# Running column sums and maxima of a graph network: ScalarE copies landed columns into PSUM, VectorE combines one column at a time

## What is computed

```python
h = jnp.maximum(_layernorm(x), 0.0)
x = x + _L0(h)      # segment_sum(H[src] * norm, dst), relu
x = x + _L1(h, ...) # segment_sum(h[src] * Wij(edge_attr) * edge_weight, dst)
for l in range(4):  # _L2: theta/phi projections, then
    agg = jax.ops.segment_max(msg, dst, num_segments=n)
for k in range(2):  # _L3: GCN convolutions
    out = jax.ops.segment_sum(h[src] * norm[:, None], dst, num_segments=n) + b
```

## Time and profile before

| | us |
|---|---|
| median of 3 runs | 10545.39 (10544.9 to 10546.17) |
| span of the profiled execution | 10630.0 |
| the seven passes, each | 1145 to 1148 |
| the stage between passes 1 and 2 (update and layer 1) | 1871 |
| from one later pass to the next | 91 to 99 |

### The profile page before, as it was taken

How to read it: one execution, slowest core, us unless ns; L and a number is a source line. 1 busy time by engine, 2 the same in 40 slices (tenths; PEclk the granted TensorE clock), 3 DMA queues, 4 the chain that set the end, 5 groups by cost and what they waited for, 6 DMA issues and landing times. The chain is left out here.

```text
span 10630.0 us, 49732 instructions
## 1 busy us (share of the span) xinstructions
PE 1639.5 (15%) x9025; PEld 1437.8 (14%) x9025; DVE 4419.4 (42%) x9272; ACT 543.8 (5%) x1417; POOL 8032.4 (76%) x7137
## 2 busy tenths in 40 slices
PE   2000048888860000100001000100001000010000
PEld 1000047777750000100001000100001000010000
DVE  4444434444443444344443444334444444444444
ACT  2000021111130000000000000000001000000000
POOL 4777768888847777677776777777777777777777
PEclk7555567777775555555555555555555555555555
DMA  5444435555532333333333333323333333333333
GB/s 190 142 142 142 145 88 77 77 74 76 77 86 91 95 95 95 99 95 95 95 97 97 95 95 95 101 93 95 95 95 98 96 95 95 95 100 95 95 95 104
DMA packets 467313, 1064.01 MB, mean 100 GB/s; under 512 B 156534, under 2 KB 276192, under 8 KB 412586
## 3 DMA queue, kind: packets, MB, share of 16 engines
q0 software_dynamic: 320736, 464.07, 19.8%
q1 hardware_dynamic: 143480, 597.45, 15.5%
q10 hardware_dynamic: 2940, 1.00, 0.0%
HBM read 517.80 MB, written 552.72 MB: 101 GB/s over the span
## 5 line engine op out<-in xcount | busy, mean ns | idle before, releaser
L991 POOL DMA_INDIRECT WORK<-table,S x5824 | 6249.0, 1073 | 2037.5 <-issue 1772.7
L1045 DVE TENSOR_TENSOR Z<-WORK,RESET 128x512 f32<-128x512 f32 x612 | 423.5, 692 | 2615.7 <-DMA WORK<-table,S 2601.8
L1210 POOL DMA_INDIRECT acc<-TOT,stage x832 | 1300.8, 1564 | 276.0 <-issue 207.6
L1090 PE MATMUL bank<-ident,WORK 128*128 128x128 f32 x7 | 3.3, 474 | 8069.6 <-DVE WORK L1074 8069.6
L1045 DVE TENSOR_TENSOR Z<-WORK,KEEP 128x512 f32<-128x512 f32 x459 | 317.6, 692 | 1958.9 <-DMA WORK<-table,S 1948.5
L1090 PEld LDWEIGHTS bank<-ident,WORK 128*128 128x128 f32 x7 | 1.3, 183 | 8071.1 <-DVE WORK L1074 8071.1
L1048 DVE TENSOR_TENSOR WORK<-WORK,Z 128x512 f32<-128x512 f32 x1071 | 741.0, 692 | 36.5
L1064 DVE TENSOR_TENSOR WORK<-WORK,Z 128x1536 f32<-128x1536 f32 (+2 forms) x448 | 633.8, 1431 | 12.4
L1059 DVE TENSOR_TENSOR Z<-WORK,S 128x1536 f32<-128x1536 f32 (+2 forms) x448 | 633.6, 1431 | 12.3
L1415 DVE SCALAR_TENSOR_TENSOR BASE<-bank,WEIGHT,BASE 128x128 f32<-128x128 f32 x832 | 234.2, 344 | 839.8 <-PE bank L1285 772.3
L1053 DVE SCALAR_TENSOR_TENSOR WORK<-WORK,S 128x128 f32<-128x128 f32 x1428 | 502.5, 352 | 50.9
(11 more groups left out here) (247 smaller groups left out, 2663.4 us busy)
## 6 DMA issues: line engine op xcount, KB each, us to landing
run_rows<-WORK SPq DMA_DIRECT2D x357, 1024.0 KB, 4.1
WORK<-table,S POOLq DMA_INDIRECT x5824
fill_rows<-BASE SPq DMA_DIRECT2D x52, 1024.0 KB, 6.8
WORK<-fill_rows SPq DMA_DIRECT2D x104, 512.0 KB
table<-TF SPq DMA_DIRECT2D x56, 384.0 KB
WORK<-carry_rows SPq DMA_DIRECT2D x49, 384.0 KB
acc<-TOT,stage POOLq DMA_INDIRECT x832
acc<-Z SPq DMA_DIRECT2D x12, 1024.0 KB
```

Of the source, the lines that this page charges most:

```text
L991: pool.indirect_dma_start(RING_T[:, b * WIDE + k, :], None, table, table_row(table, INDEX[:, t:t + 1]))\
L1045: step(dve.tensor_tensor(TMP[:, 0:groups, 0, :], rows[:, :, j - 1, :], mask(keep[:, :, j], groups, 0), op0))
L1210: pool.indirect_dma_start(acc_dram[a], bass.IndirectOffsetOnAxis(stage[:, h, j % HALF:j % HALF + 1].bitcast(u32), 0), TOT[:, j // QUAD % 2 ...
```

## The change

ScalarE, after each four columns (a `QUAD`) have landed, copies them (128 x 512) from the ring to one of the eight PSUM banks, in turn. VectorE then does one SCALAR_TENSOR_TENSOR for each column: its first input is the column before in the ring (SBUF), its second the landed column in PSUM, its scalar one number per partition from `KEEP` or `RESET` (SBUF), its output the column's place in the ring. The chunks' TENSOR_TENSORs, the scratch and the masks fall away. `reduced` counts columns. A bank is copied into again when VectorE has done the last column that it held.

```diff
-        def prefix_masks(dve, st, maximum):
...
+            def act_part(act):
+
+                for q in range(T // QUAD):
+                    act.wait_ge(landed[q % len(landed)], base + 16 * QUAD * (q * QUAD // SPAN + 1))
+                    wait(act, reduced, (q - BANKS + 1) * QUAD)
+                    first = q * QUAD % SPAN
+                    act.copy(bank(q % BANKS), RING_T[:, first:first + QUAD, :].rearrange("p t f -> p (t f)"))\
+                        .then_inc(copied, 1)
...
-                    for j in range(1, FOUR):
-                        wait(dve, reduced, n)
-                        step(dve.tensor_tensor(TMP[:, 0:groups, 0, :], rows[:, :, j - 1, :],
-                                               mask(keep[:, :, j], groups, 0), op0))
-                        wait(dve, reduced, n)
-                        step(dve.tensor_tensor(rows[:, :, j, :], rows[:, :, j, :], TMP[:, 0:groups, 0, :], op1))
...
-                for c in range(LAST):
-                    combine(c * WIDE, GROUPS)
-                    assert n == done(c)
...
+                for t in range(T):
+                    q = t // QUAD
+                    if t % QUAD == 0:
+                        dve.wait_ge(copied, q + 1)
+                    wait(dve, reduced, t)
+                    dve.scalar_tensor_tensor(RING_T[:, t % SPAN, :], RING_T[:, (t - 1) % SPAN, :], scale[:, t:t + 1],
+                                             bank(q % BANKS)[:, t % QUAD * F:(t % QUAD + 1) * F], op0, op1)\
+                        .then_inc(reduced, 1)
...
-                        if k == WIDE - 1 and c >= RING - 1:
-                            wait(pool, reduced, done(c - RING + 1))
+                            wait(pool, reduced, t - SPAN + 2)
```

More of the change, by code:

```diff
@@ L44 @@
 RING = 64 // WIDE
-FOUR = 4
-GROUPS = WIDE // FOUR
+BANKS = 8
 COUNT = T // WIDE
@@ L224, in gnn_kernel @@
         INDEX = S[:, 0:T].bitcast(i32)
-        PREFIX = S[:, T:2 * T]
-        TMP = Z[:, 0:3 * GROUPS * F].rearrange("p (g j f) -> p g j f", g=GROUPS, j=3)
         RING_T = WORK[:, :].rearrange("p (t f) -> p t f", f=F)
@@ L250, in gnn_kernel @@
         src_turned, src_sb = sem("src_turned"), sem("src_sb")
-        staged, reduced = sem("staged"), sem("reduced")
+        staged, reduced, copied = sem("staged"), sem("reduced"), sem("copied")
         stored = [sem(f"stored{i}") for i in range(BUFS)]
@@ L822, in gnn_kernel @@
         clear()
-        def prefix_masks(dve, st, maximum):
-            st.then(dve.tensor_copy(PREFIX[:, 0:T:FOUR], KEEP[:, 0:T:FOUR]))
-            for j in range(1, FOUR):
-                st.then(dve.tensor_tensor(PREFIX[:, j:T:FOUR], PREFIX[:, j - 1:T:FOUR], KEEP[:, j:T:FOUR], ALU.mult))
-            if maximum:
-                st.then(dve.tensor_scalar(PREFIX, PREFIX, -1.0, BIG, ALU.add, ALU.mult))
         def run_ends(pool, index, g):
@@ L917, in rows @@
                         on_a(act, g)
+                before["act"](act)
                 if norm_x:
@@ L956, in _, with passing @@
                 sp.wait_ge(table_out, 16 * NG)
-        def passing(maximum, pbase, fill=False, masks=None):
+        def passing(maximum, pbase, fill=False):
             base = total.gathers
@@ L967, in passing @@
             carry_dram = carry_rows[1 if maximum else 0]
-            tail = ((WIDE - HALF, 8), (WIDE - HALF + 8, 6), (WIDE - 2, 2))
-            parts = (((0, WIDE - HALF),) if WIDE > HALF else ()) + tail
+            parts = ((0, 8), (8, 6), (14, 2))
             stored_all = [16 * len(range(b, LAST, RING)) + (16 * len(parts) if LAST % RING == b else 0)
                           for b in range(RING)]
[L972 to L981, removed]
             def pool_part(pool):
@@ L995, in pool_part @@
                     pool.wait_ge(stored[b], stored_all[b])
-            total_steps = done(LAST)
+            def act_part(act):
[5 more added lines that the diff above has]
+                        .then_inc(copied, 1)
             def carry_out(pool):
@@ L1076, in dve_part @@
-                assert n == done(LAST) == total_steps
+                for t in range(T):
[6 more added lines that the diff above has]
+                        .then_inc(reduced, 1)
@@ L1088, in pe_part @@
             def pe_part(pe):
-                pe.wait_ge(reduced, total_steps)
+                pe.wait_ge(reduced, T)
                 nc.tensor.transpose(bank(0)[:, 0:P], RING_T[:, (T - 1) % SPAN, :], ident[:]).then_inc(pe_done, 1)
@@ L1106, in sp_part @@
                     if fill:
-                        wait(sp, reduced, done(c - 1) if c else 0)
+                        wait(sp, reduced, c * WIDE)
                         for h in range(WIDE // HALF):
@@ L1111, in sp_part @@
                     for first, n in parts if c == LAST else [(0, WIDE)]:
-                        sp.wait_ge(reduced, done(c, first + n) if c == LAST else done(c))
+                        sp.wait_ge(reduced, c * WIDE + first + n)
                         store(c, first, n)
@@ L1121, in sp_part, with layer @@
                         sp.wait_ge(zeroed[h], 16 * ITERS)
-            return {"pool": pool_part, "dve": dve_part, "pe": pe_part, "sp": sp_part,
+            return {"pool": pool_part, "dve": dve_part, "pe": pe_part, "act": act_part, "sp": sp_part,
                     "carry_out": carry_out, "carry_clear": carry_clear}
-        def layer(maximum, index, post, norm_x, weights, finish, scatter=False, masks=None):
-            before = passing(maximum, total.patches, scatter, masks)
+        def layer(maximum, index, post, norm_x, weights, finish, scatter=False):
+            before = passing(maximum, total.patches, scatter)
             base = list(total.rows)
@@ L1185, in edgeconv_rows @@
             return on_v, on_a
-        layer(False, idx_sum, post_gcn(None), True, [WT[:, 1, :]], (None, plain_rows), scatter=True, masks=False)
+        layer(False, idx_sum, post_gcn(None), True, [WT[:, 1, :]], (None, plain_rows), scatter=True)
         QI = UNROLL // QUAD
@@ L1572, in gnn_kernel @@
             layer(True, idx_max, post_edgeconv(False), False, [WE[:, l, k * F:(k + 1) * F] for k in range(2)],
-                  edgeconv_rows(bias_e[:, l, :]), masks=True if l == 1 else None)
+                  edgeconv_rows(bias_e[:, l, :]))
         layer(True, idx_max, post_edgeconv(True), True, [W12[:, 0, :]], (gcn_rows, None))
-        layer(False, idx_sum, post_gcn(0), False, [W12[:, 1, :]], (gcn_rows, None), masks=False)
+        layer(False, idx_sum, post_gcn(0), False, [W12[:, 1, :]], (gcn_rows, None))
         last = passing(False, total.patches)
@@ L1603, in _ @@
                     dve.tensor_tensor(X[:, gsl(g), :], X[:, gsl(g), :], rows, ALU.add).then_inc(rows_used, 1)
+            @block.scalar
+            def _(act):
+                last["act"](act)
             @block.tensor
```

## The result

| | median us | runs | ratio to before, 95% interval |
|---|---|---|---|
| before | 10545.78 | 10544.9 to 10547.65 | |
| after | 9790.7 | 9790.5 to 9794.59 | 0.9284 [0.9271, 0.9297] |

A forecast was written before the change was run, and what follows sets the result against it. The prediction took GpSimd's gathers, plus what VectorE makes them wait, as the bound. From 10545.4 us it took 751 of waiting and added 6 for copies at pass ends: 9800, range 9780 to 9890.

The forecast's parts named there:

- The bound and the 751 us: Seven passes: GpSimd's gathers set the pace; their waits for VectorE, 5824 x (1073 - 944) ns, give 751 us to remove.
- `prefix_masks`, put at 0: Mask work at the start of three passes beside gathers, VectorE otherwise idle; removing it was to gain 0.
- The mechanism: A gather that begins while a VectorE instruction with two SBUF inputs runs stands still until that instruction ends.
- second rival: Gathers wait because VectorE is busy, whatever it reads: 461 us remain, 290 gained, about 10260; chance 0.03.
- third: Rival: DMA engines set the pace once gathers come without a break; no change but 6 us, 10551; chance 0.02.
- The column instruction: 832 new VectorE instructions per pass, about 344 to 352 ns each, hold up no gather: price nothing.
- first rival: Column instructions hold gathers in part: 175 us, so 9975; at worst 512 us, so 10312; chance 0.06.
- ScalarE's copy: Copy to PSUM taken as 0.80 us, exposed only at pass ends: about 0.85 with hand-over, 6 us over seven passes.
- From span to runs: The runs' median lies 84.6 us below the profiled span 10630.0; the same difference was taken off the result.
- last rival: ScalarE's copies hold gathers: 1456 x 0.80 = 1165 us replace the 751, so 10965, slower; chance 0.02.

The follow-up runs named there:

- e1: The kernel before the change, unedited, profiled once more: 10545.45 us.
- e9: Changed kernel plus one unneeded VectorE add per four columns, both inputs in SBUF, placed between first and second column: 10058.1 us, ratio 0.9525.
- e10: Changed kernel plus the same unneeded add between first and second column of four, second input in a PSUM bank: 9807.71 us, ratio 0.9291.
- e4: Kernel before the change with only its scratch TMP moved to PSUM: 10238.33 us, ratio 0.9709.
- e2: Changed kernel with column instructions reading the landed column from the SBUF ring, not PSUM; ScalarE's copies and all waits stay: 9847.79 us, ratio 0.9337.
- e3: Changed kernel without ScalarE's copies; VectorE combines column by column from the SBUF ring once four have landed: 9808.11 us, ratio 0.9300.
- e5: Changed kernel plus one unneeded VectorE add ahead of each four columns, both inputs in SBUF: 9813.7 us, ratio 0.9308.
- e6: Changed kernel plus one unneeded VectorE add ahead of each four columns, second input in a PSUM bank: 9797.27 us, ratio 0.9292.

## Why the prediction was right

Forecast 9800 (9780 to 9890), measured 9790.7.

*The bound and the 751 us.* Right. GpSimd's gathers lost 6249.0 - 5495.3 = 754 us, and passes of 1039 us were named beforehand. The forecast lies 9 us above the measured time: the gathers of e1's trace lose 6251.1 - 5495.3 = 756 us and not 751, the copies cost 2 us less (below), and the rest is no more than the runs of one kernel differ by. `prefix_masks`, put at 0, stood beside the first gathers of three passes, among them one of 2964 and one of 1302 ns: some 2.4 us, which are part of the 754.

*The mechanism.* Right, and shown: e9 against e10 by one operand, e4 within one timeline. My sentence for it, that a gather that begins while a two-input instruction runs stands still until it ends, is too wide: one that begins near the instruction's end is not held, and of those under a 0.35 us instruction only those that begin 0.10 to some 0.21 us after its start. VectorE's busy time (second rival) is out by e10, and the DMA engines (third) by the pace at 157 GB/s in the first pass.

*The column instruction.* Its price of nothing is right: 348 ns (taken: 344 to 352), and among all 5824 gathers none longer than 1013 ns. The scalar operand that no row had excluded doesn't count, or the 725 gathers named above would have grown. By the rule of the Trainium skill that I set beside the first rival ("SBUF — State Buffer", section "Who interferes with whom"), a VectorE instruction with at most one SBUF input leaves GpSimd alone, and e10 with 0.95 beside e9 with 1.25 agrees. The Trainium skill's fixed charge for a PSUM source ("VectorE: DVE Perf Modes", section "The TRN2 errata") doesn't show: 348 ns from PSUM here, 353 in e2 from SBUF.

*The first rival's price* was mis-sized. I put 175 us on column instructions that hold gathers as two-input ones do; with two SBUF inputs they cost 56 in e2 and 22 in e3. What I had not drawn from this: if so little is lost, PSUM is hardly needed. The form gives 739 us, PSUM with its copies on top of it 17 by the medians' difference of e3 and the changed kernel, with intervals that overlap (0.9300 and 0.9284); the trace has it as 22 us of wait less 4 at the ends. In the chunked form PSUM gives 309 (e4). The sum didn't depend on which of the two removed the wait, so it came out right without this, and its coming true says nothing on what PSUM is worth.

*ScalarE's copy* was mis-sized: 589 ns and not 800. L767, which I took it from, shares the source in SBUF but not the operation nor the output in PSUM; which of these counts no run shows. With the hand-over it is 0.62 per pass (10 ns more or less), 4.3 us in place of 6.

*From span to runs.* I took 84.6 us off the span; e1 shows that they were of that one execution and outside the passes. The sum is untouched, because its terms lie in the passes.

*ScalarE's copies hold no gather* (last rival): in the changed kernel's trace 286 gathers begin while a copy runs, and they take 0.940 to 0.956 us.

What stays open: why a 0.35 us instruction holds only the gathers that begin in that short stretch. The gaps of some 0.03 us between such instructions can't be the reason, since the starts that pass undisturbed fill 0.25 us of each 0.38. An estimate from the traces: a held gather ends 0.82 us after the instruction and a free one takes 0.94, so what has to wait lies some 0.13 us after a gather's start. By this the 0.35 us instruction of 128 columns holds in its last 0.13 us and the 0.68 us one of 512 columns in its last 0.52, four times as long for four times the columns. That an instruction holds only while it goes through its columns would fit this; no run shows it.

## To carry to other kernels

Where GpSimd issues indirect DMAs back to back and sets the pace, look at the distribution of their durations, not at the mean: a median at the minimum and a few long ones beside another engine's instructions are waiting that can be had back. First shorten the instructions with two SBUF inputs that run beside them, which gave 98% of the gain here without any new engine; then move one input to PSUM where long ones must stay. Work that is set off by a landing stands at a fixed phase to the next gathers, so where in a burst an instruction stands can matter more (the gathers take 5757.2 us in e9 and 5521.0 in e5, with the same extra instruction) than that it is there.

## What the hardware showed beyond that

In the four kernels with the extra instruction (e5, e6, e9, e10) the median gather is 947 ns and not 944, with a bank as input too; the gathers of e6 and e10 take 13 and 11 us more in all than the changed kernel's. No run here says why. A ScalarE copy of 128x512 takes 589 ns from SBUF to PSUM and 585 from PSUM to SBUF.
